# Attention and gated feed-forward in one kernel: the values of every fourth step held back one step and given behind the next ones

## What is computed

```python
weights = softmax(einsum('bqhd,bkhd->bhqk', q, k) * 0.25)      # 16 heads, 1024 x 1024
out = einsum('bhqk,bkhd->bqhd', weights, v)
x = x + layernorm(concat(out) @ w_o.T)
xr, xk = mu_r*h + (1-mu_r)*h_prev, mu_k*h + (1-mu_k)*h_prev    # h = layernorm(x)
x = x + layernorm(sigmoid(xr @ W_r.T) * (square(relu(xk @ W_k.T)) @ W_v.T))
```

## Time and profile before

| | |
|---|---|
| median of 3 runs | 1273.29 us (1273.29 to 1273.8) |
| the profiled execution | 1274.69 us |
| its span on the core | 1272.9 us |
| PE / ACT / DVE / POOL busy | 98% / 84% / 61% / 22% |
| mean granted clock of TensorE | 0.998 of full speed |

### The profile page before, as it was taken

One profiled execution on the slowest core, in us unless ns is written; L12 is line 12 of the kernel. 1 busy time (PEld: TensorE's weight loads), 2 busy tenths in 40 slices (PEclk: granted clock), 3 DMA queues, 4 the chain that ended last, 5 costly groups with the idle time before them and its releaser, 6 DMA issues.

```text
span 1272.9 us, 25486 instructions
## 1 busy us (share of the span) xinstructions
PE 1252.4 (98%) x10604; PEld 603.3 (47%) x10604; DVE 779.1 (61%) x1725; ACT 1067.7 (84%) x1159; POOL 276.4 (22%) x356
## 2 busy tenths in 40 slices
PE   8999999999999999999999999999999999999997
PEld 5544454454544444454544544444444445534344
DVE  6543747758465773847567584666747466463737
ACT  4788888888888888888888888888888888898872
POOL 3000212222211321222121221223222122222211
PEclk9999999999999999999999999999999999999999
DMA  4455553317712194124733166321871129400001
GB/s 153 115 144 166 98 129 78 101 51 126 124 52 84 52 180 87 52 66 106 144 68 113 42 116 125 73 84 51 143 124 51 35 75 174 85 1 20 15 1 34
DMA packets 61797, 112.70 MB, mean 89 GB/s; under 512 B 6512, under 2 KB 31344, under 8 KB 61616
## 3 DMA queue, kind: packets, MB, share of 16 engines
q1 hardware_dynamic: 61360, 109.60, 38.8%
q10 hardware_dynamic: 288, 1.05, 0.3%
HBM read 68.42 MB, written 41.94 MB: 87 GB/s over the span
## 4 chain that ended last, share of the span: by engine, by line
PE 93%; DVE 3%; ACT 2%; DMA 1%; POOL 0%; issue 0%; ACTq 0%; DVEq 0%
PE O L602 38%; PE S L583 26%; PE M L353 14%; PE M L340 11%; PE M L250 3%; ACT PT L590 1%; DVE sth L701 1%; DMA A<-w_dram 1%; PE M L483 1%; DVE A L710 0%; PE S L1016 0%; POOL rsh L706 0%; DVE QS L474 0%; ACT QS L471 0%; DVE A L914 0%
## 5 line engine op out<-in xcount | busy, mean ns | idle before, releaser
L590 ACT ACTIVATE PT<-S 128x1024 f32<-128x1024 f32 x1024 | 1003.5, 1026 | 156.8 <-PE S L583 156.2
L602 PE MATMUL O<-PT,V 128*17 128x512 f32 x4096 | 538.9, 598 | 0.0
L583 PE MATMUL S<-QS,KS 50*128 50x512 f32 x2048 | 465.4, 450 | 3.2 <-ACT PT L590 3.2
L583 PEld LDWEIGHTS S<-QS,KS 50*128 50x128 f32 x2048 | 211.0, 183 | 452.7 <-ACT PT L590 375.2
L602 PEld LDWEIGHTS O<-PT,V 128*17 128x17 f32 x4096 | 67.8, 95 | 139.5 <-issue 137.7
L705 POOL TENSOR_SCALAR veh<-mvh 128x2 f32<-128x2 f32 x96 | 22.3, 232 | 491.3 <-DVE mvh L703 490.1
L914 DVE SCALAR_TENSOR_TENSOR A<-Z,M 128x512 f32<-128x512 f32 x30 | 20.4, 682 | 159.6 <-PE M L353 159.6
L340 PE MATMUL M<-xnT,WH 64*128 64x512 f32 (+1 forms) x504 | 110.7, 393 | 1.1 <-DVE WL L985 1.1
L353 PE MATMUL M<-WH,xnT 64*128 64x256 f32 (+1 forms) x496 | 83.0, 278 | 0.0
L353 PE MATMUL M<-WH,cT 64*128 64x256 f32 (+1 forms) x496 | 82.1, 278 | 0.5 <-DVE rec L661 0.4
L353 PE MATMUL M<-WH,C 64*128 64x256 f32 (+1 forms) x496 | 81.8, 278 | 0.0
(11 more groups left out here) (130 smaller groups left out, 1610.0 us busy)
## 6 DMA issues: line engine op xcount, KB each, us to landing
scr<-p SPq DMA_DIRECT2D x124, 256.0 KB
QS<-scr SPq DMA_DIRECT2D x56, 256.0 KB, 6.7
KS<-scr SPq DMA_DIRECT2D x56, 256.0 KB, 11.0
QS<-scr SPq DMA_DIRECT2D x70, 128.0 KB, 6.0
KS<-scr SPq DMA_DIRECT2D x68, 128.0 KB, 8.5
xA<-x_dram SPq DMA_DIRECT2D x16, 512.0 KB, 7.0
xB<-x_dram SPq DMA_DIRECT2D x16, 512.0 KB, 7.2
out_dram<-xB SPq DMA_DIRECT2D x15, 512.0 KB, 3.4
```

Of the source, the lines that this page charges most:

```text
L583: fn = lambda e, p=p, a=a, rows=rows: e.matmul(PS[p][:, a, :], KS[qd][rows, p, kt * 128:kt * 128 + 128], QS[qd][rows, p, hf * 512:hf * 512 ...
L590: e_fn = lambda e, p=p: e.activation(PT[i % 2][:, 2 * p:2 * p + 2, :], PS[p][:, :, :], ACT.Exp, scale=SCALE)
L602: fn = lambda e, j=j: e.matmul(PO[32 * j:32 * j + 17, :], V[b % 2][:, kt, 4 * qd + j, :], PT[i % 2][:, j, :], start=(kt == 0), stop=(kt == 7))
```

## The change

Steps are taken in groups of four, in all batches but the last, from step 12 of round 0 on (`paired`). In the first step of a group (s % 4 = 0) `values(i)` is held back, and `pump` is called twice: once between the two score pairs of the step, as before, and once behind the second pair. In the second step (s % 4 = 1) the held values and its own are given one behind the other, behind the second score pair. In the third step (s % 4 = 2) `pump` is not called at all: the two score pairs stand side by side, then come the values. The fourth step is as before. There are three buffers PT for the exponentials in place of two, and so the exponential of step i waits for the values of step i-3; and one buffer T in place of two. The renaming of T in the other lines is left out here.

```diff
@@ -78,7 +78,7 @@
         Z = sb("Z", [128, 2, 516])
         CC = sb("CC", [128, 2, 16, 32])
         On = sb("On", [128, 512])
-        T = [sb(f"T{i}", [128, 512]) for i in range(2)]
+        T = sb("T", [128, 512])
         cT = [sb(f"cT{i}", [128, 1024], F32R) for i in range(2)]
 
         parts = [[sb(f"p{i}{j}", [128, 512])[:, :] for j in range(2)] for i in range(2)]
@@ -87,7 +87,7 @@
 
         QS = [sb(f"QS{i}", [128, 2, 1024], F32R) for i in range(4)]
         KS = [sb(f"KS{i}", [128, 2, 1024], F32R) for i in range(4)]
-        PT = [sb(f"PT{i}", [128, 4, 512]) for i in range(2)]
+        PT = [sb(f"PT{i}", [128, 4, 512]) for i in range(3)]
         V = [sb(f"V{i}", [128, 8, 16, 17]) for i in range(2)]
         st = sb("st", [128, 8, 6])
         mv = sb("mv", [128, 8, 2])
@@ -587,9 +587,9 @@
                         pe.quiet(fn, *waits)
                     else:
                         s_of[i, p] = pe.op(fn)
-                e_fn = lambda e, p=p: e.activation(PT[i % 2][:, 2 * p:2 * p + 2, :], PS[p][:, :, :], ACT.Exp,
+                e_fn = lambda e, p=p: e.activation(PT[i % 3][:, 2 * p:2 * p + 2, :], PS[p][:, :, :], ACT.Exp,
                                                    scale=SCALE)
-                exp_of[i, p] = act.op(e_fn, s_of[i, p], pv_of.get(i - 2))
+                exp_of[i, p] = act.op(e_fn, s_of[i, p], pv_of.get(i - 3))
                 last_exp[p] = exp_of[i, p]
 
         def values(i):
@@ -600,7 +600,7 @@
                 waits.append(tk["acc_free"])
             for j in range(4):
                 fn = lambda e, j=j: e.matmul(PO[32 * j:32 * j + 17, :], V[b % 2][:, kt, 4 * qd + j, :],
-                                             PT[i % 2][:, j, :], start=(kt == 0), stop=(kt == 7))
+                                             PT[i % 3][:, j, :], start=(kt == 0), stop=(kt == 7))
                 if j < 3:
                     pe.quiet(fn, *waits)
                     waits = []
@@ -619,18 +619,18 @@
             if g == len(steps) // 8 - 1:
                 yield from last_quad(g, qd)
                 return
-            at, half = T[g % 2], qd % 2
+            at, half = T, qd % 2
             view = at[:, :].rearrange("p (y r) -> p y r", r=32)
             d = act.op(lambda e: e.activation(On[:, :], PO[:, :], ACT.Copy), pv_of[8 * g + 7], tk.get("On_read"))
             tk["acc_free"] = d
             yield REST
-            d = dve.op(lambda e: e.transpose(at[:, :], On[:, :]), d, tk.get(("T", g % 2)), split_of["wr"])
+            d = dve.op(lambda e: e.transpose(at[:, :], On[:, :]), d, tk.get("T"), split_of["wr"])
             tk["On_read"] = d
             d = dve.op(lambda e: e.reciprocal(rec[:, :], view[:, :, 16]), d, tk.get("rec_read"))
             over = rec[:, :].unsqueeze(2).to_broadcast([128, 16, 16])
             d = dve.op(lambda e: e.tensor_tensor(CC[:, qd // 2, :, 16 * half:16 * half + 16], view[:, :, 0:16], over,
                                                  ALU.mult), d, tk.get("CC_read"))
-            tk["rec_read"] = tk["T", g % 2] = d
+            tk["rec_read"] = tk["T"] = d
             if not half:
                 return
             yield REST
@@ -1091,8 +1092,23 @@
                         alone(0, -1, word)
 
                 age = 2 if b + 1 == B and s < (5 if hf else 20) else 1
-                pump(0 if u == 0 and s < 9 else 32 - s, age, (lambda: scores(i + 1, 1)) if nxt else None)
-                values(i)
+
+
+
+                paired = b + 1 < B and (u > 0 or s >= 12)
+                late = (lambda: scores(i + 1, 1)) if nxt else None
+                if not (paired and s % 4 == 2):
+                    pump(0 if u == 0 and s < 9 else 32 - s, age, late)
+                    if paired and s % 4 == 0:
+                        pump(32 - s, age)
+                elif late:
+                    late()
+                if paired and s % 4 == 0:
+                    held.append(i)
+                else:
+                    for k in (*held, i):
+                        values(k)
+                    held.clear()
                 go = 2
                 for work in rested[:go]:
                     until_rest(work)
```

More of the change, by code:

```diff
@@ L158, in sandwich_kernel @@
         load_weights(sp, xb_flat[1], "wkf", "wvf")
-        load_weights(sp, T[0], "wr")
+        load_weights(sp, T, "wr")
         rows_of_quad = [None, None]
@@ L642, in quad @@
                                                     ALU.subtract), d)
-            tk["T", g % 2] = tk["cT", g // 4, qd // 2, 0] = tk["cT", g // 4, qd // 2, 1] = d
+            tk["T"] = tk["cT", g // 4, qd // 2, 0] = tk["cT", g // 4, qd // 2, 1] = d
         def last_quad(g, qd):
-            at, half, parts_of = T[g % 2], qd % 2, [{}, {}]
+            at, half, parts_of = T, qd % 2, [{}, {}]
             for h, got in enumerate(parts_of):
@@ L655, in turned @@
                 x = got["cols"]
-                got["T"] = dve.op(lambda e: e.transpose(at[:, x], On[:, x]), got["On"], tk.get(("T", g % 2)))
+                got["T"] = dve.op(lambda e: e.transpose(at[:, x], On[:, x]), got["On"], tk.get("T"))
             def divided(got):
@@ L1069, in sandwich_kernel @@
         split_weights(["wq", "wk"])
+        held = []
         for u in range(2 * B):
```

## The result

1343.03 us (median of 4 runs, 1340.4 to 1344.15) against 1273.55 (4 runs): ratio 1.054, 95% interval 1.0522 to 1.0558. The profiled execution took 1342.46 us with a span of 1340.7. The prediction had the sign, the mechanism at y0's bank, and less than a third of the size: +19 us forecast, +69 measured, above the range.

The account below looks back on a forecast made before the run. PE, busy 98% of the span, was taken as the bound; -33 (saving) + 13 (turned blocks) + 26 (y0's bank) + 10 (bank behind) + 3 (tanh) = +19 us: median 1292 us, range 1279 to 1306, 80% range 1256 to 1308.

Parts of the forecast that it names:

- What bounds the kernel: Whole kernel: PE sets the time, busy 98% of the span, and waits for hardly anything.
- the saving: Fewer turns of PE's array in each group of four: 0.30 us a group, 109 groups, -33 us (-21 to -38).
- The bank of y0: Steps 8 to 11, rounds 1 to 13: PE waits 2.0 us for a bank behind DVE's normalisations, +26 us.
- the bank behind it: Next group, 13 rounds: a block waits 0.7 us for a bank that a late DVE split frees, +10 us (0 to +17).
- the search for waits: Blocks' waits on DVE were priced only at y0's bank (+26 us) and the next bank (+10 us).
- Turned blocks: Steps with transposed tiles: second score pairs wait for exponentials; 1.9 us per even round, 0.25 per odd, +13 us.
- Tanh: Step 23 of odd rounds: tanh and a copy on ACT make the next group's scores 0.4 us late, +3 us.
- rival (b): ACT becomes the bound, each group's fourth step waiting for exponentials: 1308 us in the middle, 1320 at the far end; chance 0.12.
- (a): Banks are free in time, so both bank terms go: -17 us, 1256 us; chance 0.23.

Follow-up runs that it names:

- f1: The changed kernel with only the last two groups of a round (steps 24 to 31) in fours: 1268.88 us, ratio 0.9959.
- h1: Changed kernel, rested works ahead of the second pump, fours only in groups 1, 4, 6, 7 (even rounds), 0, 1, 4, 6, 7 (odd), round 0 from step 24: 1263.66 us.
- h2: The changed kernel with only steps 24 to 31 and steps 8 to 11 of a round in fours: 1307.11 us, ratio 1.0263.
- e4: The changed kernel, but steps 20 to 23 of the even rounds as before the change: 1318.73 us, ratio 1.0359.
- e2: The changed kernel, with the works that rested before the step given ahead of the first step's second pump: 1334.16 us, ratio 1.0477.
- h3: The changed kernel with only steps 24 to 31 of a round and steps 0 to 3 of even rounds in fours: 1282.33 us, ratio 1.0068.
- e1: The changed kernel with values held and three buffers, but one pump in every step as before the change: 1297.06 us, ratio 1.0186.

## Why the prediction was wrong, by its steps

- **What bounds the kernel; the saving:** right. Score pairs between halves at 0.24 us, values at 1.84 for 1.87, and ACT's layout held (one gap a group, D's scores in time). Only the score pair ahead of both values costs 0.07 more than the sum had; f1 and h1 show 0.18 to 0.26 us a group for 0.30, and in steps 4 to 7 of odd rounds h1 gains nothing.
- **The bank of y0:** right in place, mechanism and size of the wait (11.12 for 11.11). The term was too small by the clock: no term for a falling clock stands anywhere in the prediction, though it had PE standing for 2 us 13 times. Here that is 8 x 1.6 = 13 us (some 9 once the shorter groups behind are counted), in h2 nine falls, in e4 three.
- **The step that failed:** the search for waits. It asked only at y0 and at the bank behind it what stands ahead in DVE's queue, and followed that queue to 13 us behind step 8 and no further. The same question was not put to steps 16 to 23 nor to v1 in step 0, whose groups it entered with the saving alone. Even steps 20 to 23 measured 26.5 us above its figure (4.8 of them falls of the clock), odd steps 4 to 7 and 16 to 19 together 10.8. With the 12.3 in steps 8 to 11 that is the whole miss of 50 us; the other rows cancel. e2, e4 and h3 show what was there in its place: a block that ends in A's second pump overtakes the works that rested, and behind it DVE or POOL is late for a later block. e2 also shows a second part that no order cures: PE comes sooner to a queue that is still full.
- **Turned blocks and the bank behind:** the split ends at 13.0 us for 13.15 by hand, and the wait is 0.57 for 0.7, but in only 5 of the 13 rounds, since a fall of the clock takes its place in the others. That is most of why steps 12 to 15 came to 7.6 and not 14. Even steps 0 to 3 were somewhat dearer (0.57 a group by hand, 0.77 measured).
- **Tanh:** right in place, 0.25 us a round for 0.4 (9.47 against 9.22 for the same group in f1).
- **The range and two sums:** the range of 1279 to 1306 is not the bounds of the terms. Added up as they stand, they give 1261 to 1320. That 1343 lies above even this says that terms were missing and not only mis-sized. In rival (b) the far end should take 109 x 0.2 = 22 us and not 16. The upper bound of 0.35 us for a group's saving does not follow from waves of 0.43 (0.19 + 1.97 - 1.72 = 0.44). Neither bears on the miss.
- **Rivals:** (a) held that with y0's normalisations ahead of y1's statistics both bank terms go. e2 puts them there: y0's bank is free in time, but the wait at the bank behind it grows to 2.5 us. f1 and h1 reach its kind of time (no new waits) only by leaving steps 8 to 11 as they were. (b), ACT as the bound, did not come: scores waited for exponentials 10.4 us in all, 34 times, against 3.2 us in 10 times before. The Trainium skill's rule (TensorEngine Tiling (Array Packing), PSUM Bottleneck) that PSUM's emptying may become the limit has no support in the changed kernel, where ACT's busy share fell to 78%; in e1, where exponentials have less room, scores wait for them 126 times, 30.5 us in all.

Open: why the score pair ahead of two values costs 0.40 us, behind which of two equal waits the clock falls, and how k1's wait divides between the order and DVE's load (e2 leaves 1.06 of 2.3 us, with other times around it).

## What to carry to other kernels

When work is moved to an earlier place in the program, look at every in-order queue that it is put into, on every engine: what it now overtakes is late, and whoever waits for that may be PE. A rule that counts steps does not keep a distance in time once steps are uneven. Take the new order only where the trace shows room (h1: 61 groups of 109, 0.7% faster) and allow for a fall of the clock behind each wait of PE near 2 us as well (here behind 3 to 9 of 13 equal waits); and when one wait is taken away, ask what its delay was hiding.

## What the hardware showed that was not expected

- Behind waits of 1.7 us on PE that the trace shows as equal, the clock fell in 8 of 13 rounds (9 in h2, 3 in e4), each time for 1.6 us of lost time in that group.
- Two groups of column-quarter products in a row lose nothing between them: 16 records in 1.84 us, 0.46 a wave.
- A cast of 512 columns on DVE out of SBUF takes longer when it starts while POOL works on 512 columns. DVE's timeline of round 4, after:

```profile
400.55 0.43 DVE L378 CAST C<-A 128x512 fp32r<-128x512 f32 x1
...
401.63 0.98 DVE L378 CAST cT<-T 128x512 fp32r<-128x512 f32 x1
```

and POOL's:

```profile
401.06 1.27 POOL L783 TENSOR_TENSOR C<-A,C 128x512 fp32r<-128x512 f32 x1 [2.21 <-DVE C L378]
402.69 1.74 POOL L641 TENSOR_TENSOR cT<-T,cT 128x512 fp32r<-128x512 f32 x1 [0.36 <-DVE cT L378]
```

0.43 us before POOL starts, 0.98 beside it, and 1.40 for the cast at 403.31, which lies within POOL's second operation; that one took 1.74 where h3's took 1.27. In the changed kernel's trace all 22 casts that start so take 0.98 to 1.41 us, and the same casts of cT and B alone 0.43 (39 times); beside POOL's small root (L398, 4 columns) a cast keeps its 0.43. The long casts are part of the backlog on which k1 waits, but the kernel before has 30 of them (1.00 at 384.37, 1.40 at 386.07), so they don't explain the difference. No run took POOL's work away, so this is read from the overlap alone.
